# Keys, values and mask of a masked cross-attention made at the end of the sublayer before, a split first tile, and loads moved between stores

## The reference, cut to what matters

```python
def L0_attn(x):                       # head mixing: each token attends over its own 16 heads
    q = x @ Wq + bq                   # (B, T, 16, 16)
    kv = (x @ Wdown + bdown) @ Wup + bup
    k, v = split(kv)                  # the latent x @ Wdown has 64 features
    att = softmax(einsum('bthd,btgd->bthg', q, k) / 4)
    return einsum('bthg,btgd->bthd', att, v) @ Wout + bout

def L0_xattn(x, ctx, mask):           # masked heads: 77 context rows, keys and values from ctx alone
    q, k, v = x @ Wq.T + bq, ctx @ Wk.T + bk, ctx @ Wv.T + bv
    s = where(mask == 0, -1e9, q @ k.T / 4)
    return softmax(s) @ v @ Wo.T + bo

def L0_ffn(x): ...                    # feed-forward with ternary weights and 8-bit activations

def L1_attn(x):                       # paged attention, 64-token pages, rotated queries and keys
    ...
```

## Time and profile before

| | |
|---|---|
| median of 3 runs | 2747.84 us (2745.88 to 2752.18) |
| the profiled execution's own time | 2748.86 us |
| its span | 2747.1 us |
| TensorE matmul busy | 2432.6 us (89%) |
| VectorE busy | 1438.9 us (52%) |
| ScalarE busy | 946.2 us (34%) |
| GpSimd busy | 494.6 us (18%) |
| mean granted TensorE clock | 0.937 of full speed |

### The profile page before, as it was taken

How to read it: one execution, slowest core, us unless ns; L and a number is a source line. 1 busy time by engine, 2 the same in 40 slices (tenths; PEclk the granted TensorE clock), 3 DMA queues, 4 the chain that set the end, 5 groups by cost and what they waited for, 6 DMA issues and landing times. The chain is left out here.

```text
span 2747.1 us, 36310 instructions
## 1 busy us (share of the span) xinstructions
PE 2432.6 (89%) x14259; PEld 1686.0 (61%) x14259; DVE 1438.9 (52%) x2474; ACT 946.2 (34%) x1799; POOL 494.6 (18%) x422
## 2 busy tenths in 40 slices
PE   6986767778889879979999998889999799999888
PEld 3665654422224768856667667757776577777764
DVE  7996979367773421036564653651110455455543
ACT  3443657225554213234442431311111322122132
POOL 3442320220001124310100011122221311001010
PEclk8998989969999979999999999779999899999999
DMA  3003100373420046622322230322231300000000
GB/s 113 1 1 122 48 32 1 58 145 50 69 44 26 5 173 226 226 89 89 93 71 65 67 98 0 104 58 101 77 90 56 103 18 18 12 18 12 1 33 31
DMA packets 77659, 181.47 MB, mean 66 GB/s; under 512 B 16935, under 2 KB 41128, under 8 KB 71945
## 3 DMA queue, kind: packets, MB, share of 16 engines
q1 hardware_dynamic: 64596, 126.74, 16.7%
q0 software_dynamic: 10368, 50.01, 5.3%
q10 hardware_dynamic: 2542, 2.62, 0.3%
HBM read 149.51 MB, written 25.43 MB: 64 GB/s over the span
## 5 line engine op out<-in xcount | busy, mean ns | idle before, releaser
L1655 PE MATMUL L_ffn_h_ps<-L_ffn_xgT,L_ffn_w 128*128 128x512 f32 (+2 forms) x992 | 231.9, 390 | 4.0 <-DVE L_ffn_xgT L1738 2.3
L1667 PE MATMUL L_ffn_y_ps<-L_ffn_w,L_ffn_h 128*128 128x256 f32 x1008 | 222.5, 380 | 4.8 <-issue 3.9
L1713 ACT ACTIVATE L_ffn_h<-L_ffn_h_ps,L_ffn_w 128x640 f32<-128x640 f32 (+2 forms) x184 | 101.6, 553 | 346.1 <-PE L_ffn_h_ps L1655 335.0
L527 DVE TENSOR_REDUCE L_attn_neg<-L_attn_Y 128x1 f32<-128x512 f32 (+3 forms) x304 | 187.4, 657 | 55.8 <-PE L_attn_Y L400 54.4
L1667 PEld LDWEIGHTS L_ffn_y_ps<-L_ffn_w,L_ffn_h 128*128 128x128 f32 x1008 | 189.9, 190 | 32.9 <-issue 8.3
L1655 PEld LDWEIGHTS L_ffn_h_ps<-L_ffn_xgT,L_ffn_w 128*128 128x128 f32 x992 | 153.8, 192 | 81.5 <-issue 66.8
L497 ACT ACTIVATE L_attn_room<-L_attn_Y 128x1024 f32<-128x1024 f32 (+1 forms) x192 | 147.4, 812 | 81.1 <-PE L_attn_Y L451 80.5
L400 PE MATMUL L_attn_Y<-L_attn_K,L_attn_Q 104*128 104x512 bf16 (+3 forms) x384 | 119.6, 363 | 44.9 <-DVE L_attn_neg L527 35.9
L1747 DVE TENSOR_TENSOR L_ffn_yg<-L_ffn_y_ps,L_ffn_w 128x256 f32<-128x256 f32 x63 | 26.7, 425 | 223.5 <-PE L_ffn_y_ps L1667 223.5
L1738 DVE COPY L_ffn_xgT<-L_ffn_t_ps 128x256 f32<-128x256 f32 x63 | 24.5, 421 | 212.1 <-PE L_ffn_t_ps L1642 211.7
L1788 POOL DMA_INDIRECT token_outputs<-L_ffn_yg,puts x63 | 61.8, 982 | 324.5 <-DVE L_ffn_yg L1747 324.5
(11 more groups left out here) (577 smaller groups left out, 5099.3 us busy)
## 6 DMA issues: line engine op xcount, KB each, us to landing
L_ffn_w<-in_L_ffn_w SPq DMA_DIRECT2D x8, 2180.0 KB
L_attn_bc<-decays SPq DMA_DIRECT2D x32, 512.0 KB, 6.1
L_attn_bp<-decays SPq DMA_DIRECT2D x32, 256.0 KB, 7.0
L_attn_Q<-L_attn_q_parts SPq DMA_DIRECT2D x48, 128.0 KB, 4.7
L_attn_K<-L_attn_k_parts SPq DMA_DIRECT2D x48, 128.0 KB, 7.6
L_attn_first_w<-in_L_attn_w SPq DMA_DIRECT2D x8, 640.0 KB
L_attn_w<-in_L_attn_w SPq DMA_DIRECT2D x8, 640.0 KB, 3.8
L_attn_v_all<-zero SPq DMA_DIRECT2D x1, 4096.0 KB, 22.5
```

The source lines that it names most:

```text
L527: nc.vector.tensor_reduce(neg[:, c, j0:j0 + heads, tt], R[n % 2][:, 0:heads * width(tt, c)].rearrange("p (h k) -> p h k", h=heads), X_AXIS ...
L1655: ins = nc.tensor.matmul(h_ps[f % 2][:, lo // CW, 0:hi - lo], w1[g % NB][:, kt, f * P:(f + 1) * P], xgT[u][:, kt, lo:hi], start=kt == 0, s ...
L1667: ins = nc.tensor.matmul(y_ps[k % 2][:], h[:, f, t * P:(t + 1) * P], w2[g % NB][:, f, :], start=f == 0, stop=f == FT - 1)
L1713: nc.scalar.activation(h[:, f, 0:n], h_ps[f % 2][:].rearrange("p c n -> p (c n)")[:, 0:n], func, bias=b1[g % NB][:, f:f + 1]).then_inc(sem ...
```

## The change

Four edits:
1. **Head mixing's start.** Seven products on a tile of zeros, whose result nobody reads, go ahead of TensorE's wait for weights; ScalarE takes an exponential of a constant ahead of its own, which puts the table load there. The first 512 latent columns are made in two pieces (`PIECES`): tile 0's 128 ahead of its queries, the other 384 behind its keys and values.
2. **Keys, values and mask of masked heads** are made by a new class. Its 16 products stand in TensorE's queue in iteration 13 of head mixing, behind `project(11)` and ahead of the turns of unit 2, in the banks of latents, queries and keys/values. VectorE's eight instructions stand at the end of iteration 16, behind the sum of unit 6 and ahead of the division of tile 15. Masked heads then begin with `queries(0)`. The results lie in tiles of their own, allocated earlier.
3. **The quantized feed-forward** takes one half of three double buffers, or both, from tiles that masked heads have finished with, to make room.
4. **Paged attention's SP queue:** the loads of slots 0, 1 and 2 move from between batch 0's stores to ahead of batch 1's stores of parts 0, 1 and 2, one each.

```diff
             for b in range(B):
                 for r in range(NR):
+                    if b == 1 and r < SLOTS:
+                        sp.wait_ge(stored[r // 2], 16 * NR)
+                        load(sp, r)
                     sp.wait_ge(part_done[2], b * NR + r + 1)
                     for g in range(2):
...
-                    if b == 0 and r >= 2:
-                        for slot in range(2 * r - 4, min(2 * r - 2, SLOTS)):
-                            sp.wait_ge(stored[slot // 2], 16 * NR)
-                            load(sp, slot)
...
+        PIECES = (0, P, CW, 2 * CW, 3 * CW, N)
+        piece = lambda n: 0 if n == 0 else n // 4 + 1
...
         def _(pe):
+            for _ in range(7):
+                nc.tensor.matmul(y_ps[:, 0, :], core.zero[:, 0:P], core.zero[:], start=True, stop=True)
             pe.wait_ge(loaded, ALL)
 
             def latents(c):
-                pe.wait_ge(core.x_loaded, 16 * (c + 1))
+                lo, hi = PIECES[c:c + 2]
+                pe.wait_ge(core.x_loaded, 16 * max(1, c))
...
-                    mm = nc.tensor.matmul(lat_ps[0:LAT, :], wdown[:, kt, :], xT[:, kt, c * CW:(c + 1) * CW], start=kt == 0, stop=kt == KT - 1)
+                    mm = nc.tensor.matmul(lat_ps[0:LAT, 0:hi - lo], wdown[:, kt, :], xT[:, kt, lo:hi], start=kt == 0, stop=kt == KT - 1)
...
-                pe.wait_ge(lat_ready, n // 4 + 1)
+                pe.wait_ge(lat_ready, piece(n) + 1)
...
             latents(0)
             front(0)
+            latents(1)
             front(1)
             front(2)
...
                 if k >= 2:
                     project(k - 2)
+                if k == NT_ - 3:
+                    pe.wait_ge(q_ready, NT_)
+                    pe.wait_ge(kv_ready, NT_)
+                    made.products(pe, lat_ps[:], (q_ps[:], kv_ps[:]))
                 for g in TURNS.get(k, ()):
                     tail.turn(pe, g)
...
+            nc.scalar.activation(warm[:], core.one[:], ACT.Exp)
             act.wait_ge(loaded, ALL)
...
             latents(0)
             queries_keys_values(0)
+            latents(1)
             queries_keys_values(1)
...
                     tail.add(dve, (k - 4) // 2)
+                if k == NT_:
+                    made.make(dve, lat_ps[:], (q_ps[:], kv_ps[:]))
             tail.add(dve, 7)
...
             queries(0)
             queries(1)
-            pe.wait_ge(k_ready, 1)
             scores(0)
-            pe.wait_ge(v_ready, 1)
...
+class MaskedKeys:
+    def products(self, pe, k_bank, v_banks):
+        nc, w = self.nc, self.early.tiles
+        pe.wait_ge(self.early.loaded, self.early.all)
+        for mt in range(KT):
+            for kt in range(KT):
+                nc.tensor.matmul(k_bank[:, mt * B * S2:(mt + 1) * B * S2], w["kw"][:, kt, mt * P:(mt + 1) * P], w["ctxT"][:, kt, :],
+                                 start=kt == 0, stop=kt == KT - 1)
+        for b in range(B):
+            for kt in range(KT):
+                mm = nc.tensor.matmul(v_banks[b][0:S2, :], w["ctxT"][:, kt, b * S2:(b + 1) * S2], w["vw"][:, kt, :],
+                                      start=kt == 0, stop=kt == KT - 1)
+        mm.then_inc(self.multiplied, 1)
+
+    def make(self, dve, k_bank, v_banks):
+        nc, w = self.nc, self.early.tiles
+        dve.wait_ge(self.early.loaded, self.early.all)
+        nc.vector.tensor_scalar(self.fill[:], w["mask"][:], 0.0, None, ALU.not_equal).then_inc(self.keep_set, 1)
+        dve.wait_ge(self.multiplied, 1)
+        for mt in range(KT):
+            for h in range(2):
+                nc.vector.tensor_scalar(self.kz[:, mt, :, h, :], k_bank[:, mt * B * S2:(mt + 1) * B * S2].rearrange("p (b k) -> p b k", b=B),
+                                        w["kb"][:, mt:mt + 1], w["pair"][:, h:h + 1], ALU.add, ALU.mult).then_inc(self.made, 1)
+        for b in range(B):
+            nc.vector.tensor_tensor(self.v[:, b, :], v_banks[b][0:S2, :], w["vb"][0:S2, :], ALU.add).then_inc(self.made, 1)
+        dve.wait_ge(self.keep_set, 1)
+        nc.vector.tensor_scalar(self.fill[:], self.fill[:], -1.0, -MASKED, ALU.add, ALU.mult).then_inc(self.made, 1)
```

More of the change, by code:

```diff
@@ L731, in _ @@
                     if (k + 3) % 4 == 0:
-                        latents((k + 3) // 4)
+                        latents(piece(k + 3))
                     front(k + 3)
@@ L887, in _, with masked_heads_stage @@
                     tail.shift(pool, g)
-def masked_heads_stage(nc, core, early, bit, values):
+def masked_heads_stage(nc, core, early, bit, values, made):
     A = core.A
@@ L1148, with bit_ffn_stage @@
 ROUND = 1.5 * 2.0 ** 23
-def bit_ffn_stage(nc, core, weights, values, following):
+def bit_ffn_stage(nc, core, weights, values, following, made):
     F = 1024
@@ L1168, in bit_ffn_stage @@
         xr = [m.sb(f"xr{u}", [P, QT, D]) for u in range(2)]
-        xq = [m.sb(f"xq{u}", [P, QT, D], BF16) for u in range(2)]
+        xq = [m.sb("xq0", [P, QT, D], BF16), made.early.tiles["qw"][:].rearrange("p k n -> p (k n)").bitcast(BF16).rearrange("p (t d) -> p t d", d=D)]
         xqT = m.sb("xqT", [P, KT, N], BF16)
@@ L3507, in build @@
     masked, bit = masked_early(nc, early, A), BitWeights(nc, early, A)
+    made = MaskedKeys(nc, early, masked)
     late, ffn = ExitStack(), []
```

56 lines of the change are left out of this document (20 added, 36 removed).

## The result

In six runs each the changed kernel takes 2736.84 us (median; 2728.59 to 2743.77) and the kernel before 2750.01 us (2745.88 to 2759.99). The recorded ratio is 0.9936, 95% interval 0.9917 to 0.9955. Against the 2747.84 us that the prediction started from, the change gives 11.0 us; by the two medians 13.2 us; by the ratio, which is not the quotient of the medians (that is 0.9952), 17.6 us, 12.4 to 22.8. 15.0 were forecast. So whole times confirm a gain and bound its size loosely; how large each part is, the timelines have to show. A second series gave a ratio of 0.9943 (0.9925 to 0.9961).

The account below looks back on a forecast made before the run. Bound, read per place: the engine wait that ends last, at four places in the first four stages. 3.6 + 4.7 - 0.9 + 7.6 = 15.0 us off 2747.84 gave 2732.8; range 2727 to 2739, with rivals 2726 to 2740.5.

Parts of the forecast that it names:

- Start: Head mixing's start: VectorE's first head product, at 15.83 us before, comes 3.6 us earlier; range 0.4 to 3.8.
- The fallback of 2.1: Head mixing's start: if TensorE's clock rises only at 12 us, the gain is 2.1 us instead of 3.6.
- The phase of GpSimd: Head mixing, VectorE's product for tile 4: could give back or take up to 3 us; taken as 0.
- Inserted products: End of head mixing: 16 products take 4.6 us, VectorE waits 1.0, cost 0.9; 0 at best, 5.6 at low clock.
- Keys, values and mask: Start of masked heads: VectorE's first softmax 4.7 us earlier; 3.5 if low clock holds, 6.5 at high clock throughout.
- lower-clock rival: Head mixing: start stays slow (2.1 us for 3.6), inserted products at low clock (5.6 for 0.9); 2739 us; chance 0.13.
- Loads between stores: Paged attention's projections: storing batch 0's part 3 ahead of loads brings VectorE's last rotation 7.6 us earlier; 0 to 8.4.
- batch 1's part 0: Paged attention: if the store of this part lands after 564.3 us, only part 2 is late, not VectorE.
- clock luck: Elsewhere in the kernel: moves forecast or rivals by a few us; three earlier runs span 2745.88 to 2752.18.
- the store was no gate: Paged attention's projections: another wait ends at the same place, 7.4 us remain, 2740.4 us; chance 0.07.
- Slower, another table: Masked heads and head mixing: first exponential picks another table; 2753 us and more, some 20 worse with drains; chance 0.02.
- Start slow and products at low clock: Head mixing's start gains 2.1 us for 3.6, inserted products cost 5.6 for 0.9; 2739 us; chance 0.13.

Follow-up runs that it names:

- e4 to e6: Changed kernel without, one each: unread products, split latents, early exponential; first latent product to first head product 7.03, 5.43, 4.33 us, against 4.15.
- e4: Changed kernel without the seven unread products at its start; first latent product to VectorE's first head product 7.03 us, against 4.15.
- e8: Changed kernel with all three slot loads issued together ahead of batch 1's first store; 2743.61 us against 2737.71, last rotation 69.91 us behind the first page load.
- e1: Kernel before with one edit alone: SP's slot loads put between the stores of batch 1; 2749.55 us, ratio 0.9976.
- e3: Kernel before with the middle edit alone: keys, values and mask of masked heads made while head mixing ends; 2748.31 us, ratio 0.9980.

## Why the prediction was right

- *Start*: 3.6 said, 3.5 measured; what it was made of I knew less well. e4 to e6 price the edits, each taken out alone: unread products 2.9 (1.9 with an earlier rise of the clock), split 1.3, table load 0.2; they overlap and don't add up to 3.5. The fallback of 2.1 (clock rising late) didn't occur: in all ten profiles with the unread products VectorE had started by 12.35 (13.45 without the split). In the one execution without them the gain was 0.65 (7.68 - 7.03). The latents themselves took 0.65 us for the 0.46 that I put in. The phase of GpSimd, taken at 0, gave back 0.5 us at tile 4 (5.07 us for 5.54).
- *Inserted products*: 4.6 us said, 4.5 measured; wait of VectorE 1.0 said, 0.76; cost 0.9 said, 0.86 measured. The step that failed is beside it. I had seen that the projection at 221.70 would come later, and costed it as a delay only; it also lengthened TensorE's idle time from 2.77 to 3.20 us, and behind it the mixing sum took 1.4 us more. I had allowed for the low clock on the sum of tile 13 alone, where it would be hidden; that sum ran at the upper level and tile 14's did not. Whether the products caused this stays open (5 of 8 against 1 of 6). By the lower-clock rival 5.6 us would have been paid; 2.3 were, if the 1.4 are counted here.
- *Keys, values and mask*: 4.7 said, 5.1 measured: TensorE's hand-overs are shorter than the 0.2 that I allowed, and scores took 1.41 of my 1.6. VectorE's part lay in the idle time named, with 1.63 us of it left (1.4 said).
- *Loads between stores*: 7.6 said; the last rotation came 7.95 earlier in the whole change and 7.58 in the edit alone. The mechanism named, one store behind 24 loads, is right. So was what I said of batch 1's part 0, that a late store would hold up part 2 and not VectorE; e8 bears it out, and its expectation, which had the last rotation wait for that store, was wrong.
- *Sum*: at the last rotation the changed kernel is 14.1 us ahead, of the 15.0 forecast; the parts missed by 1.6 us one way (1.4 of it tile 14's sum) and by 0.8 the other, so the closeness of the sum is in part luck. From there to the end it keeps 11.2: 1.9 are lost in the stages up to 1216 and 1.1 behind. The second profile is 14.8 ahead at the last rotation, 15.8 at 1216 and 11.3 at the end. These stages hold none of the change, and which clock they get differs between executions of one and the same kernel: the changed kernel's series ran from 2728.59 to 2743.77. The prediction had this as clock luck, of either sign; here it took.
- *Rivals*: "the store was no gate" fell by e1. "Slower, another table" fell at 3.46: the table loaded for the exponential serves the biases behind it, and the start has no other load. Its price with a drain was summed wrong: a drain as long as the load is 2 x 1.28 us more on each of sixteen tiles, some 41 us and not 20; nothing hung on it. "Start slow and products at low clock" occurred in neither half.

## What to carry to other kernels

Read a queue's order for the one transfer that somebody waits for, and put it ahead of the bulk; how the bulk is spaced behind it may matter nothing. When work is put into an idle engine ahead of a hand-over, put it behind that hand-over if it can stand there: the same sixteen products cost 0.9 us of VectorE's time ahead of the transposes and none behind them. A gain of 2 to 5 us that a timeline proves at its place need not reach the end of a 2.7 ms kernel: look at the next long stage for what meets what.

## What the runs showed of the hardware

- TensorE's clock at a start, by the durations: idle until about 8 us, it ran the next products at the lower level until about 12 (e3, before), 14 (e1) or 16 us (e4); after 14 unread products (1.85 to 6.6) and 1.6 us of idle time it stood at the upper level. At the end of head mixing, waits of 0.70 and 0.94 us with products between them kept the granted clock at 1.00 into the next stage, where waits of 3.29 and 1.57 us had let it fall to 0.50 (249 to 256 us of the changed kernel).
- VectorE and GpSimd: a 128x32 operation that takes 0.19 us took up to 2.4 when GpSimd's 128x1024 product of 2.36 us ran, whether it had two inputs in SBUF (L533, L538) or was a cast (L536). The Trainium skill (SBUF — State Buffer, SBUF: two separate sides) calls it an exclusive lock held for the whole instruction, and the trace agrees.
- The 234 us stretch of paged attention goes with two counts in the table: with four blocked operations it takes 233.7 to 234.1 us with the clock low for 7 or 10 us, 234.9 to 235.5 with 14, 236.5 with 17; with two more blocked operations it takes 3.2 us more at 7 us of low clock and 3.6 at 17. No run sets either count by itself, so this is what goes together, and not shown to be the cause.
